# Later steps for the second-half projections, the values and y of a batch, and the parts of the negated maxima on GpSimd

## The reference

```python
q, k, v = heads(xn @ Wq), heads(src @ Wk), heads(src @ Wv)      # 16 heads of 16
weights = softmax(mask_or_nothing(q @ k.T / 4))                 # 512 x 512 per head
y = merge(weights @ v) @ Wo                                     # then y is added to x, or normed and added
```

## Time and profile before

| | |
|---|---|
| median of three runs | 2344.68 us |
| profiled execution | 2349.11 us, of which span 2346.9 us, mean granted clock of PE 0.962 |
| PE busy (its ends are modelled) | 2145.7 us, 91% |
| DVE, ACT, POOL busy | 1329.3, 1129.8, 665.2 us |
| attention, first to last exponential | 594.2 to 1722.8 us |
| stages before / after | start to 547 us / 1760 us to the end |

### The profile page before, as it was taken

How to read it: one execution, slowest core, us unless ns; L and a number is a source line. 1 busy time by engine, 2 the same in 40 slices (tenths; PEclk the granted TensorE clock), 3 DMA queues, 4 the chain that set the end, 5 groups by cost and what they waited for, 6 DMA issues and landing times. The chain is left out here.

```text
span 2346.9 us, 33103 instructions
## 1 busy us (share of the span) xinstructions
PE 2145.7 (91%) x10551; PEld 1202.2 (51%) x10551; DVE 1329.3 (57%) x3625; ACT 1129.8 (48%) x2079; POOL 665.2 (28%) x671
## 2 busy tenths in 40 slices
PE   6897899994999999999999999999959999999995
PEld 2474466661333323333334343344337888888884
DVE  5456543312877777777777777777874542112125
ACT  2233311121788888888766556666622222222233
POOL 3210233334111011111134233343223334333342
PEclk9898999995999999999999999999979999999998
DMA  5325444335433332422344242543226666667684
GB/s 177 128 99 196 135 110 110 94 65 113 94 61 72 63 55 48 74 52 31 39 55 62 39 55 38 65 61 41 28 64 189 189 184 193 187 189 207 190 278 124
DMA packets 198072, 249.77 MB, mean 106 GB/s; under 512 B 26592, under 2 KB 176096, under 8 KB 195872
## 3 DMA queue, kind: packets, MB, share of 16 engines
q1 hardware_dynamic: 176320, 217.96, 37.2%
q0 software_dynamic: 20736, 29.15, 7.1%
q10 hardware_dynamic: 864, 0.79, 0.3%
HBM read 162.77 MB, written 46.53 MB: 89 GB/s over the span
## 5 line engine op out<-in xcount | busy, mean ns | idle before, releaser
L2395 ACT ACTIVATE att_prob<-att_ps 128x512 f32<-128x512 f32 x1024 | 587.6, 597 | 267.2 <-PE att_ps L2235 184.7
L2542 DVE CUSTOM_DVE_ANT_0 att_junk<-att_pm,bias 128x512 bf16<-128x512 f32 x512 | 337.0, 685 | 154.3 <-PE att_pm L2218 153.8
L2538 DVE TENSOR_REDUCE att_tops<-att_pm 128x1 f32<-128x512 f32 x512 | 340.0, 683 | 119.8 <-PE att_pm L2218 117.5
L1529 POOL DMA_INDIRECT sum<-exL_ys,exL_put x106 | 176.8, 1668 | 395.8 <-DVE exL_ys L1731 224.0
L2253 PE MATMUL att_po<-att_prob,att_vals 128*32 128x512 f32 x2048 | 277.1, 613 | 1.0 <-ACT att_prob L2395 1.0
L2218 PE MATMUL att_pm<-att_kstack,head_qstack 96*128 96x512 bf16 x512 | 205.5, 403 | 21.4 <-DMA head_qstack<-att_q 19.5
L2235 PE MATMUL att_ps<-att_qstack,att_kstack 99*128 99x512 bf16 x512 | 195.6, 385 | 17.1 <-ACT att_prob L2395 6.5
L2235 PE MATMUL att_ps<-head_qstack,att_kstack 99*128 99x512 bf16 x512 | 198.0, 387 | 9.5 <-ACT att_prob L2395 3.6
L2218 PE MATMUL att_pm<-att_kstack,att_qstack 96*128 96x512 bf16 x512 | 196.5, 384 | 10.4 <-DMA att_qstack<-att_q 8.1
L1622 ACT ACTIVATE exL_hid<-exL_ph,head_b 128x256 f32<-128x256 f32 (+1 forms) x160 | 73.3, 459 | 195.7 <-PE exL_ph L1580 193.8
L1622 ACT ACTIVATE exL_hid<-exL_ph,exL_b 128x256 f32<-128x256 f32 (+1 forms) x152 | 71.2, 469 | 189.5 <-PE exL_ph L1580 187.7
(11 more groups left out here) (427 smaller groups left out, 3436.4 us busy)
## 6 DMA issues: line engine op xcount, KB each, us to landing
head_qstack<-in_L_W SPq DMA_DIRECT2D x40, 1024.0 KB
exL_w<-in_L_W SPq DMA_DIRECT2D x38, 1024.0 KB
early_w<-in_L_W SPq DMA_DIRECT2D x16, 1024.0 KB, 5.5
att_qstack<-att_q SPq DMA_DIRECT2D x96, 128.0 KB, 5.3
att_kstack<-att_k SPq DMA_DIRECT2D x96, 128.0 KB, 4.6
head_qstack<-att_q SPq DMA_DIRECT2D x90, 128.0 KB, 5.8
att_kstack<-kstack SPq DMA_DIRECT2D x32, 256.0 KB, 5.0
kstack<-early_k SPq DMA_DIRECT2D x24, 256.0 KB
```

Of the source, the lines that this page charges most:

```text
L1529: pool.indirect_dma_start(out=sums[0], out_offset=bass.IndirectOffsetOnAxis(ap=put[slot][:, c:c + 1], axis=0), in_=ys[slot][:, c, :], in_o ...
L2395: act.activation(prob[i % PROBS][:], ps[i % 2][:], ACT.Exp, scale=SCALE).then_inc(s["p_ready"], 1)
L2538: ins = dve.tensor_reduce(tops[g % 2][:, t, j:j + 1], pm[i % TOPS][:], AX.X, ALU.max)
L2542: ins = dve.tensor_tensor_reduce(junk[:, i % TOPS, :], pm[i % TOPS][:], G["bias"][0][:, t, :], 1.0, -BIG / 2, ALU.add, ALU.max, tops[g % 2 ...
```

## The change

- **Job table.** Where the next batch is self attention, `k1 q1 v0 v1` move from steps 21, 24, 27, 30 to 31, 34, 40, 43; where it is cross attention, `q1` moves from 18 to 33. `y0 y1` of the batch before move from 11 and 14 to 24 and 27 (next batch self) or 42 and 46 (next batch cross); in the last batch they stay. `u0 u1` move from 47 and 50 to 49 and 52 except in the last batch.
- **SP.** `fill` 1 comes before storing rows and probabilities.
- **POOL.** `cut_maxima` is POOL's: five instructions on 128 x 4 x 4 elements in place of DVE's four. They stand before `norm` (round 1's maxima), before `cut` 0 (round 2's), behind `norm_y` (round 3's) and behind `add_y` (round 0's of the next batch). `add_y` moves behind `cut` 1.
- **DVE.** `cut_maxima` is gone from the batches (only the one ahead of batch 0 stays). At the first step of a round `max_step` waits until POOL has split the maxima that `tops` held two rounds before. `y_stats` moves from steps 25 to 28 to steps 29 to 32, `y_chunk` from 33 to 36 to steps 36 to 39, except in the last batch.

```diff
--- before.py
+++ after.py
@@ -1809,13 +1809,15 @@
     if next_self is not None:
         jobs += [(11, "a", "turn0+"), (13, "a", "turn1+"), (55, "d", "neg0+")]
     if next_self:
-        jobs += [(15, "a", "k0+"), (18, "a", "q0+"), (21, "a", "k1+"), (24, "a", "q1+"), (27, "a", "v0+"), (30, "a", "v1+")]
+        jobs += [(15, "a", "k0+"), (18, "a", "q0+"), (31, "a", "k1+"), (34, "a", "q1+"), (40, "a", "v0+"), (43, "a", "v1+")]
     elif next_self is False:
-        jobs += [(15, "a", "q0+"), (18, "a", "q1+")]
+        jobs += [(15, "a", "q0+"), (33, "a", "q1+")]
     if prev_self is not None:
-        jobs += [(4, "d", "out3-"), (7, "a", "att0-"), (9, "a", "att1-"), (11, "d", "y0-"), (14, "d", "y1-")]
+        y0, y1 = {None: (11, 14), True: (24, 27), False: (42, 46)}[next_self]
+        jobs += [(4, "d", "out3-"), (7, "a", "att0-"), (9, "a", "att1-"), (y0, "d", "y0-"), (y1, "d", "y1-")]
     if prev_self:
-        jobs += [(47, "a", "u0-"), (50, "a", "u1-"), (57, "d", "logits-")]
+        u0, u1 = (47, 50) if next_self is None else (49, 52)
+        jobs += [(u0, "a", "u0-"), (u1, "a", "u1-"), (57, "d", "logits-")]
     return sorted(jobs)
 
 
@@ -2112,12 +2114,13 @@
                         fill(w, 1 - par, 0)
                     negatives(par, 2, w.index("d", "neg2"))
                     negatives(par, 3, w.index("d", "neg3"))
+                    if not w.last:
+                        fill(w, 1 - par, 1)
                     if w.prev_self:
                         store_rows(w.prev)
                         if w.prev.rows:
                             store_prob(w.prev.rows - 1)
                     if not w.last:
-                        fill(w, 1 - par, 1)
                         negatives(1 - par, 0, w.index("d", "neg0+"))
 
                 def behind(last, after):
@@ -2410,9 +2413,34 @@
             def _(pool):
                 chain = Chain(pool, s["pchain"])
 
-                def cut(w, o):
+                def cut_maxima(of, g, jobs):
+
+                    top, done = tops[g % 2], of.number * NG + g
+                    pool.wait_ge(s["m_done"], past(of.number * PER + (g + 1) * ROUND))
+                    pool.wait_ge(s["neg_ready"], past(done))
+                    pool.wait_ge(s["job_d"], past(jobs))
+                    alone(pool)
+                    chain(pool.tensor_scalar(neg3[:, :, 0, :], top[:], -1.0, None, ALU.mult))
+                    chain(pool.tensor_tensor(rest[:], top[:], neg3[:, :, 0, :], ALU.add))
+                    chain(pool.tensor_scalar(neg3[:, :, 1, :], rest[:], -1.0, None, ALU.mult))
+                    chain(pool.tensor_tensor(rest[:], rest[:], neg3[:, :, 1, :], ALU.add))
+                    pool.tensor_scalar(neg3[:, :, 2, :], rest[:], -1.0, None, ALU.mult).then_inc(s["neg_ready"], 1)
+
+                def maxima_due(w, g):
+
+                    if g == 0:
+                        if not w.first:
+                            cut_maxima(w.me, 1, w.base("d"))
+                    elif g < NG - 1:
+                        cut_maxima(w.me, g + 1, w.index("d", f"neg{g}") + 1)
+                    elif not w.last:
+                        cut_maxima(w.next, 0, w.index("d", "neg3") + 1)
+
+                def cut(w, o, kinds="kq"):
 
                     for n in cuts_of(w.next.self_):
+                        if n not in kinds:
+                            continue
                         x_, (hi, mid, lo) = full[n][:, o, :], (p[:, o, :] for p in parts[n])
                         pool.wait_ge(s["free_a"], past(w.index("a", f"{n}{o}+") + 1))
                         if not w.start:
@@ -2478,14 +2506,20 @@
                     clear(1)
 
                 def batch(w, par):
+                    maxima_due(w, 0)
                     if not w.last:
                         norm(w.next)
+                    maxima_due(w, 1)
+                    if not w.last:
                         cut(w, 0)
                     if w.prev_self:
                         norm_y(w.prev)
-                        add_y(w.prev, 1 - par)
+                    maxima_due(w, 2)
                     if not w.last:
                         cut(w, 1)
+                    if w.prev_self:
+                        add_y(w.prev, 1 - par)
+                    maxima_due(w, 3)
                     if w.next_self:
                         keep(w.next, 1 - par)
 
@@ -2533,6 +2567,10 @@
 
                 def max_step(of, g, n):
                     i, t, j = g * ROUND + n, n // HG, n % HG
+                    if n == 0 and of.number * NG + g > 1:
+
+                        dve.wait_ge(s["neg_ready"], past(of.number * NG + g - 1))
+                        alone(dve)
                     dve.wait_ge(s["m_ps"], past(of.number * PER + i + 1))
                     if of.self_:
                         ins = dve.tensor_reduce(tops[g % 2][:, t, j:j + 1], pm[i % TOPS][:], AX.X, ALU.max)
@@ -2741,14 +2779,6 @@
                 def batch(w, par):
                     for g in range(NG):
                         for n in range(ROUND):
-                            if 1 <= n <= 4:
-
-                                if g == 0 and not w.first:
-                                    cut_maxima(w.me, 1, w.base("d"), n - 1)
-                                elif 0 < g < NG - 1:
-                                    cut_maxima(w.me, g + 1, w.index("d", f"neg{g}") + 1, n - 1)
-                                elif g and not w.last:
-                                    cut_maxima(w.next, 0, w.index("d", "neg3") + 1, n - 1)
                             if not w.last and g == 0 and 1 <= n <= CB:
                                 norm_chunk(w, n - 1)
                             if not w.last and g == 0 and 7 <= n < 7 + CB:
@@ -2767,10 +2797,11 @@
                                     dve.wait_ge(s["job_a"], past(w.index("a", "att1-") + 1))
                                 job(w.of(name), name, w.index("d", name))
                             if w.prev_self:
-                                if g == 1 and 9 <= n < 9 + CB:
-                                    y_stats(w.prev, w.index("d", "y1-"), n - 9)
-                                if g == 2 and 1 <= n <= CB:
-                                    y_chunk(w.prev, n - 1)
+                                at, spread, scaled = g * ROUND + n, 25 if w.last else 29, 33 if w.last else 36
+                                if spread <= at < spread + CB:
+                                    y_stats(w.prev, w.index("d", "y1-"), at - spread)
+                                if scaled <= at < scaled + CB:
+                                    y_chunk(w.prev, at - scaled)
                                 if (g, n) == (3, 15):
                                     router(w.prev)
                             if g < 2:
```

## The result

| | median (us) | lowest to highest | runs |
| --- | --- | --- | --- |
| before | 2343.92 | 2338.68 to 2350.02 | 6 |
| after | 2331.08 | 2326.29 to 2335.29 | 6 |

Ratio after to before 0.9944, 95% interval 0.9931 to 0.9957: 0.56% faster. Forecast were 2340 us and a range of 2322 to 2358. The time lies in the range, 8.9 us under the forecast, and within 1.1 us of rival A (2330). Of A's three conditions two came true (the split ends before k0 is there, and the clock did not fall behind the new wait); the third, that DVE is not held, came true in its cost alone: DVE is held, and PE does not feel it.

A forecast was written before the change was run, and what follows sets the result against it. PE was taken as the bound, busy nine tenths of attention. Terms -9.8, +2.2, +0.4, -3.0, +1.8 and +3.4 sum to -5.0 us against the 2344.7 us median: 2340 us, range 2322 to 2358.

The forecast's parts named there:

- rival A: More gain stays: split ends before k0 is there, clock never falls, DVE not held; -14.4 us, 2330 us, chance 0.22.
- three signs of being wrong: Round 1 shorter than 21 us, cross batches changing by over 1 us, or POOL's split far from 1.7 us.
- what it said would be seen: Step 63 waits gone, new 1.5 to 2.5 us wait at round 2, round 1 21.9 us, round 0 15.7.
- (1): Second fill, batches 9 to 14: lands near 26 us into round 2, so step 63's 2.5 us wait goes.
- (2): First fill, batches 8 to 14: chain of 12 DMAs; PE, with 19.6 us work in round 1, waits about 1.5.
- (3): POOL's split ahead of the first cut takes 1.7 us and starts it 0.7 late; round 1 takes 21.9 us.
- (8): Lower clock behind the new 2.2 us wait, batches 8 to 14: two of seven at 1.7 us, +3.4.
- (4): Batches 9 to 14: 71.3 us each against 72.9, -9.8 in all; batch 8 +2.2, batch 7 +0.4.
- (5): Cross batches 1 to 6: q1's move 0, y's -0.5 a batch, -3.0 for six; no wait for the fill.
- (6): DVE without its four split instructions a round: worth 0, bounds 0 and -0.3 us a batch.
- (7): y_chunk's scalings at steps 36 to 39 wait behind POOL's cuts: +0.3 us a batch, +1.8 for six.
- Rival C: y_chunk held each time for the longest cut instruction, 1.2 us: +16 in place of +1.8, 2354 us, chance 0.10.

The follow-up runs named there:

- the order alone: Kernel before with add_y behind the second cut and fill 1 ahead of the row stores; no jobs moved, split on DVE: 2331.51 us, ratio 0.9963.
- the last kernel above: Order, cross moves, POOL's split, second cut behind first, self jobs unmoved; then cross q1 at step 31, last batch's rank_head(0) at step 40: 2318.19 us.
- the longer split: Kernel after with seven more small POOL instructions in the split ahead of the first cut: 2358.55 us, ratio 1.0081.
- The moves alone: Moves of jobs, y_stats and y_chunk: the kernel after with DVE's split, 2339.88 us, set against the order alone, 2331.51 us.
- the cross moves alone: Kernel before with only the cross batches' q1, y0 and y1 moved: 2339.2 us, ratio 0.9986.
- the two with DVE's split: Kernel after with DVE splitting the maxima again, run twice: 2339.88 us, ratio 0.9989, and 2335.45 us, ratio 0.9976.
- both cuts first: Kernel before with POOL doing both cuts before norm_y and add_y, and fill 1 ahead of the row stores: 2326.55 us, ratio 0.9928.

## Why the prediction was right or wrong, step by step

The forecast was right in its range and in most of its mechanism. Its own narrower range, 2333 to 2348, was missed by 2 us: by its bound for "faster", under 2333, the kernel is just faster, to which it gave 0.30. None of its three signs of being wrong came; of what it said would be seen, the new wait is too short (1.0 to 1.4 us, not 1.5 to 2.5), and so is round 1 (21.1 to 21.5, not 21.9). That the time lies so close to rival A is partly luck: A puts attention 14.4 us down and it is 12.5, with misses on both sides that cancel.

(1) *Second fill early*: right. The earlier trace rows have no successor in the trace of after: the last DMA of the second fill lands 26.9 us into round 2 of batch 10 (forecast near 26), with over 34 us to the next batch, and the order alone takes 13.2 us out of batches 9 to 14. The clock's falls behind the old wait went with it.

(2) *First fill becomes the wait*: right in kind and place. The landing 20.5 us into the round is within 0.1 of the forecast chain without its delay. Too small was PE's own work, 20.6 us and not 19.6, since y0 in step 24 stands behind `neg2`'s copy and `y_stats` stands between the reductions of step 31. So the idle was shorter on both counts.

(3) *POOL's split 0.7 us late*: wrong, and with (8) the step that failed. Its length was right (1.55 us, forecast 1.7). Its start was not: in after, the last reduction of round 0 is done about 0.5 us before the first exponential of round 1, and not 0.5 after it. The split is over 0.70 us before k0 in each of batches 8 to 14, and 1.1 before it in batch 7, so its delay is 0. Round 1 is 21.10 to 21.47, not 21.9.

(4) *Batches 9 to 14*: round 0 15.4 to 15.9 (forecast 15.7), rounds 2 and 3 34.3 (33.7; u at steps 49 and 52 makes round 3 0.86 us longer than with the order alone, 14.75). The sum itself has a slip: 1.6 times six is 9.6, not 9.8. Batch 8 +1.4 and not +2.2, batch 7 -0.4 and not +0.4, as round 1 is shorter in both.

(5) *Cross batches*: y's -0.56 against a forecast -0.5. q1's move was put at 0 and is -0.27: its two pieces cost 1.29 us in round 1 and 1.02 in round 2. Six times this is 1.6 of the 2.1 us missed. The wait for DVE of the earlier trace rows has no part in it; it is still there in batch 3 of after, and goes only in the last kernel above, with q1 in step 31:

```profile
828.72 0.39 PE L2221 MATMUL att_pm<-att_kstack,head_qstack 96*128 96x512 bf16 x1 [0.57 <-DVE att_tops L2580]
```

(6) *DVE without its split*: put at 0, with a bound of 0.3 a batch. It is worth 4.1 to 4.5 us by the profiles, 4.7 by the times, some 0.6 a batch. DVE's queue is the limit in a few steps only (6, 7 and 40), and the working looked for whole rounds.

(7) *`y_chunk` beside the cuts*: the scaling is stretched as forecast (median 0.64 us, up to 1.39, in place of 0.41), yet round 2 holds 18.73 in every batch, in batch 8 too, which has no `y_chunk`: +1.8 was 0. The q1 and v0 jobs stand in the same steps; that they are the cover is argued, not tested. Without these jobs there, in the kernel with the order alone, the same costs 1.08 us a batch. Rival C's mechanism is thus real, and its price hangs on what else PE has to do there. The Trainium skill, page "SBUF — State Buffer", section "Who interferes with whom", says that where DVE and GpSimd want the ports they share, the one that issues first holds them for its whole instruction and the other is blocked. The trace of the order alone fits this in kind: the 1.26 us scaling starts 0.05 us behind POOL's instruction and ends 0.15 us after it. That the ports are the cause, no run here singles out.

(8) *The clock*: +3.4 was 0. The reason given, a wait of 2.2 us as long as the old one, fell with (2) and (3): it was 1.0 to 1.4. The longer split, which brings the wait back to 2.4 to 3.2 us, brings the falls back too, six of seven.

In sum, 12.5 us of attention against a forecast 5.0: 1.6 mostly by (3) in batches 7 and 8, 2.6 in batches 9 to 14 (that is (3), (7) and (8), 8.7 together, less 0.7 a batch for (4) and 1.5 for the clock's fall in batch 11), 2.1 by (5), and 1.2 in batches 0 and 15, which differ by as much between profiles of like kernels.

About half of what the order gave in self batches was taken back: it alone gives 13.2 us in batches 9 to 14, and in after 5.9 of this are lost again, and 1.4 in batch 8. Of the 5.9, 1.5 is the fall in batch 11. The moves alone cost 8 to 10 us there; POOL's split returns some 4.

## What to carry to other kernels

When a fill is late, look first at what stands ahead of it in the queues of the engines that make and issue it. Moving two calls was worth at least as much here as a new table of jobs, and moved jobs mostly shift work between rounds that are both full. Time a released engine from the instruction that releases it, not from the start of a round: one microsecond there (0.5 before it, not 0.5 after) decided whether a step was hidden. A wait can have a price in clock beside its length, so halving it can save more than half, and a forecast should carry both levels of the clock.

## What the runs showed of the hardware

- The granted clock behind idle PE. Of 19 waits of 2.3 to 3.2 us in batches 8 to 14 (six in before, six with the cross moves alone, seven with the longer split) 13 were followed by 3.4 or 6.8 us at the 1.2 GHz level (granted clock 0.5), some from just before the wait's end; 6 were not. Of 28 waits of 0.9 to 1.5 us (after, its second profile and the two with DVE's split) none was. The wait of 5.0 us at step 47 of batch 15 is in eleven profiles, each time with such a fall. What decides between the 13 and the 6 is open.
- A fall without a wait. In six of the twelve profiles the clock fell once for 3.4 us in step 60 of one of batches 9 to 13, with no idle of PE over 0.1 us in the 8 us ahead of it. In batch 11 of after (length, busy PE, weight loads, DVE, ACT, POOL, clock):

```profile
1427.00:1431.00 4.00, 3.93 (x16) 0.79 (x15) 2.46 (x7) 1.69 (x3) 0.00 (x0) 0.65 0.00 0
```

  It costs about 1.5 us; its cause is open.
- DVE and POOL. A 128 x 256 scaling on DVE took 0.40 to 0.42 us alone (72 of them in before, with the cross moves alone and with both cuts first) and up to 1.39 beside POOL's cuts, and POOL's cast of 0.61 took 0.76 where it started 0.11 us behind a scaling: both sides pay.
- Small POOL instructions of 128 x 16 take 0.22 to 0.28 us with 0.08 to 0.09 between them, of one or two inputs alike.
